# A graph layer's source terms: seven gathers per pair, the eighth tile by columns and rows, with a table made on chip

## What is computed

```python
msg_in = jnp.concatenate([x[src], x[dst], edge_attr_32], axis=-1)
messages = relu(msg_in @ mW1 + mb1) @ mW2 + mb2
aggregated = jax.ops.segment_sum(messages, dst, num_segments=12500)
upd_in = jnp.concatenate([x, aggregated], axis=-1)
y = x + relu(upd_in @ uW1 + ub1) @ uW2 + ub2
return layernorm(y)          # per node, no scale or shift, eps 1e-5
```

## Time and profile before

| | us |
|---|---|
| median of 3 runs (1914.49 to 1922.07) | 1921.44 |
| the profiled execution | 1922.22 |
| its span | 1920.4 |
| DVE busy | 1540.8 (80%) |
| POOL busy | 1431.4 (75%) |
| PE busy (matmuls) | 1429.3 (74%) |
| ACT busy | 1242.0 (65%) |
| DMA moved | 229.86 MB, 44% of the engines' time in the middle |

### The profile page before, as it was taken

One profiled execution on the slowest core, in us unless ns is written; L12 is line 12 of the kernel. 1 busy time (PEld: TensorE's weight loads), 2 busy tenths in 40 slices (PEclk: granted clock), 3 DMA queues, 4 the chain that ended last, 5 costly groups with the idle time before them and its releaser, 6 DMA issues.

```text
span 1920.4 us, 56413 instructions
## 1 busy us (share of the span) xinstructions
PE 1429.3 (74%) x8716; PEld 1334.2 (69%) x8716; DVE 1540.8 (80%) x10793; ACT 1242.0 (65%) x10165; POOL 1431.4 (75%) x1527
## 2 busy tenths in 40 slices
PE   6776677777678777767768777776867878777877
PEld 6776566777667677666667667766767767766776
DVE  5568888888888888888888888888888888888883
ACT  3246766767766766766666666766666666766663
POOL 7777777777777777777777777777777777777773
PEclk8898888778877878788887887878788776877686
DMA  9664444444444444444444444444444444444441
GB/s 239 163 154 113 123 114 114 123 115 114 123 113 114 124 115 112 120 118 113 115 123 113 112 122 117 114 119 120 112 115 123 113 114 122 115 114 119 118 109 35
DMA packets 169379, 229.86 MB, mean 120 GB/s; under 512 B 98508, under 2 KB 117687, under 8 KB 168701
## 3 DMA queue, kind: packets, MB, share of 16 engines
q1 hardware_dynamic: 112484, 124.14, 23.4%
q0 software_dynamic: 48416, 97.68, 20.6%
q10 hardware_dynamic: 8254, 5.59, 1.2%
HBM read 217.59 MB, written 9.60 MB: 118 GB/s over the span
## 4 chain that ended last, share of the span: by engine, by line
POOL 63%; issue 23%; PE 4%; DVE 3%; DMA 3%; DVEq 1%; ACT 1%; POOLq 1%; SPq 1%; ACTq 0%
POOL gath L717 63%; DVE col_x L469 2%; DMA gath<-table_src,idx 1%; PE ps_sum L856 1%; DVEq L460 1%; DMA table_src<-gath 1%; PE ps_pre L824 1%; PE ps_pre L825 1%; DVE hid L1180 1%; PE ps_pre L790 0%; PE ps_pre L832 0%; POOLq L302 0%; DMA xwin<-in_xT_dram 0%; ACT hid L1000 0%; DMA col_src<-in_srcT_dram 0%
## 5 line engine op out<-in xcount | busy, mean ns | idle before, releaser
L717 POOL DMA_INDIRECT gath<-table_src,idx x1388 | 1309.6, 944 | 423.0 <-issue 420.6
L469 ACT COPY col_x<-xdeg 64x1 f32 x9428 | 912.4, 187 | 237.6 <-issue 219.6
L832 PE MATMUL ps_pre<-rhs,lhs 128*128 128x128 f32 x3226 | 603.0, 363 | 448.3 <-DVE lhs L1158 445.6
L469 DVE COPY col_x<-xdeg 64x1 f32 x9408 | 718.2, 138 | 216.0 <-issue 215.5
L832 PEld LDWEIGHTS ps_pre<-rhs,lhs 128*128 128x128 f32 x3226 | 558.8, 269 | 477.1 <-DVE lhs L1158 473.9
L856 PE MATMUL ps_sum<-onehot,hid 128*128 128x96 f32 x3322 | 473.2, 304 | 13.0 <-ACT rhs L976 11.9
L856 PEld LDWEIGHTS ps_sum<-onehot,hid 128*128 128x128 f32 x3322 | 463.3, 221 | 23.5 <-issue 15.2
L1007 ACT ACTIVATE hid<-hid 128x1024 f32<-128x1024 f32 x202 | 212.5, 1052 | 180.4 <-DVE hid L1180 177.0
L1180 DVE TENSOR_TENSOR hid<-ps_pre,gath 128x1024 f32<-128x1024 f32 x202 | 246.4, 1220 | 87.2 <-DMA gath<-table_src,idx 75.4
L1158 DVE TENSOR_SCALAR_CACHE_REDUCE lhs<-lhs,place 96x1024 f32<-96x1024 int32 x208 | 264.6, 1272 | 32.7 <-PE ps_sum L765 19.8
L1150 DVE TENSOR_TENSOR onehot<-ps_iota,dst_rel 128x768 f32<-128x768 f32 (+1 forms) x209 | 196.9, 943 | 0.1
(11 more groups left out here) (109 smaller groups left out, 639.1 us busy)
## 6 DMA issues: line engine op xcount, KB each, us to landing
lhs<-in_dst_dram SPq DMA_DIRECT2D x207, 384.0 KB
lhs<-in_edgeT_dram SPq DMA_DIRECT2D x207, 128.0 KB
gath<-table_src,idx POOLq DMA_INDIRECT x1388
table_src<-gath SPq DMA_DIRECT2D x12, 512.0 KB, 7.0
xwin<-in_xT_dram SPq DMA_DIRECT2D x208, 24.0 KB
idx<-in_srcT_dram SPq DMA_DIRECT2D x192, 4.0 KB
out_dram<-yout ACTq DMA_DIRECT2D x48, 64.0 KB, 1.6
col_src<-in_srcT_dram SPq DMA_DIRECT2D x148, 0.5 KB
```

The lines of the kernel that those rows point to most:

```text
L469: ins = copy(col_x[:, i, start + n + j:start + n + j + 1], col)
L717: pool.indirect_dma_start(gath[0:m, k, j * H:(j + 1) * H], None, table_src, src_by_tile(p, k, j, m)).then_inc(gathered[k], 16)
L832: mm = nc.tensor.matmul(to[0:m, j * H:(j + 1) * H], lhs[:, k, j * P:j * P + m], rhs[:, k, :], start=True, stop=not by_cols)
```

## The change

- **Programs.** `pairs` writes all iterations out for all engines; no loop is left.
- **Gathers.** All source numbers are loaded once into `idx_all` (pairs 0 to 15 early as before, the rest by one DMA); `idx` and its loads at each step go. From pair 13 to 206 every pair has seven gathers, slot 0 too. The last pair keeps three.
- **Eighth tile.** Its 128 edges are split: 8 by rows, 64 columns by ACT, 56 by DVE (24 and 32). For the rows SP issues eight DMAs per pair, each one row of `table_src` (512 B) into one partition of `gath`'s eighth tile, whose other partitions are set to zero once per slot; the first 8 columns of `col_x` are zero. `add_gathered` waits for the rows and adds eight tiles, as before.
- **Numbers.** `col_src` and its DMAs go. At steps 6 to 8 DVE copies the eighth tiles' numbers out of `idx_all`, PE turns them by two transposes, and DVE writes them as integers to `col_tab`, columns 8 to 127 multiplied by 4, so that they are byte offsets into `xdeg`. `column` uses them without a multiplication. `COL_GROUP` is 6.
- **Register loads.** ACT loads 16 at a time, the first 16 of a pair a step ahead; DVE 24 and 32; SP 8. The window's starts are loaded four at a time by DVE (`load_starts`) and SP.
- **Order.** At step p ACT copies all 64 columns of pair p + 2, after relu. DVE copies 32 of pair p + 1 between onehot and the compare, and 24 of pair p + 2 at the end; the addresses for the sums are resolved (`place_sums`) ahead of the first batch. SP issues the rows of p + 3 last, behind a wait for `hsum_made` of p - 1.

The diff, cut to its core:

```diff
-PEELED = 4
-COL_K = (1, 2, 3)
-COL_FIRST = 3
+EARLY = 16
+COL_FROM = 13
 COL_TILE = PT - 1
-COL_HALF = P // 2
-COL_GROUP = 3
-COL_PLAN = (((2, 0, 32), (1, 48, 16)), ((2, 32, 32), (0, 0, 16)), ((0, 16, 32), (0, 48, 16)), ((1, 0, 32), (1, 32, 16)))
-COL_BATCHES = (3, 3, 2)
+COL_ROWS = 8
+COL_ACT = 64
+COL_LOAD = 16
+COL_DVE = 24
+COL_GROUP = 6
+DVE_FROM = COL_ROWS + COL_ACT
+WORD = 4
+COL_MADE = 6
+TAB = (PAIRS + 2) // 2
 LAST_ROWS = TILES - 1
-LAST_COLS = ((2, LAST_ROWS, P), (0, TILES, TAIL))
...
-        def pairs(eng, step, node, tail, peeled=PEELED, looped=True):
-
-
-            for it in range(peeled if looped else LAG):
+        def pairs(eng, step, node, tail):
+            for it in range(ITERS - 1):
...
+        def gathers_of(p):
+            return rows_of(p) if is_last(p) else PT - has_cols(p)
...
+        def load_regs(eng, p, start, count):
+            row, half = p % TAB, p // TAB
             regs = [eng.alloc_register(f"col{next(col_regs)}") for n in range(count)]
+            for n in range(0, count, 32):
+                eng.load(regs[n:n + 32], col_tab[row:row + 1, half, start + n:start + min(n + 32, count)])
+            return regs
+        def column(eng, reg, scaled):
+            if not scaled:
+                return xdeg[0:D, bass.ds(eng.snap(reg, donate=True, min_val=0, max_val=N - 1), 1)]
+            at = eng.snap(reg, donate=True, min_val=0, max_val=(N - 1) * WORD, out_of_modulus=WORD)
+            return xdeg[0:D, :].bitcast(U8)[:, bass.ds(at, WORD)].bitcast(F32)
+        def copy_batch(eng, copy, k, start, regs):
+            for n in range(0, len(regs), COL_GROUP):
+                of = [column(eng, reg, start + n + j >= COL_ROWS) for j, reg in enumerate(regs[n:n + COL_GROUP])]
                 for col in of:
                     eng.lower_ap(col)
                 for j, col in enumerate(of):
+                    ins = copy(col_x[:, k, start + n + j:start + n + j + 1], col)
+            return ins
+        def wait_cols(eng, p):
+            if p == COL_FROM:
+                eng.wait_ge(cols_tabled, 4)
+            if col_before(p) is not None:
+                eng.wait_ge(pe_steps, steps_for_pre(col_before(p)))
+            let(eng)
+        def src_by_tile(p, j, m):
...
+                if (it, k) == (0, 2):
+                    sp.dma_start(idx_all[:, EARLY * PT:], srcT[:, EARLY * PT:PAIRS * PT]).then_inc(idx_last_in, 16)
                 if pair(it, k, -SLOTS):
                     load_window(*pair(it, k, -SLOTS))
                 if pair(it, k, -PREP):
                     load_pair(*pair(it, k, -PREP))
+                p = it * SLOTS + k
+                if has_rows(p + PREP):
+                    load_rows(p + PREP, (k + PREP) % SLOTS)
+            def load_rows(p, k):
+                if p == COL_FROM:
+                    sp.wait_ge(cols_tabled, 4)
+                sp.wait_ge(hsum_made, p - SLOTS + 1)
+                if not has_rows(p - SLOTS):
+                    sp.wait_ge(gath_zero, p - COL_FROM + 1)
+                let(sp)
+                for n, reg in enumerate(load_regs(sp, p, 0, COL_ROWS)):
+                    src = sp.snap(reg, donate=True, min_val=0, max_val=N - 1)
+                    sp.dma_start(gath[n:n + 1, k, COL_TILE * H:PW], table_src[bass.ds(src, 1), :]).then_inc(rows_in[k], 16)
...
-                if not (isinstance(p, int) and p < RAW + SLOTS):
+                if p >= RAW + SLOTS:
                     pool.wait_ge(hsum_made, p - SLOTS + 1)
-                if not p_early(p):
-                    pool.wait_ge(idx_in[k], (it - PEELED + 1) * 16)
+                if p == EARLY:
+                    pool.wait_ge(idx_last_in, 16)
                 let(pool)
-                for j, m in tiles_of(p):
-                    if j == rows_of(p) or j == COL_TILE and has_cols(it, k):
-                        break
-                    pool.indirect_dma_start(gath[0:m, k, j * H:(j + 1) * H], None, table_src, src_by_tile(p, k, j, m)).then_inc(gathered[k], 16)
+                for j, m in tiles_of(p)[0:gathers_of(p)]:
+                    pool.indirect_dma_start(gath[0:m, k, j * H:(j + 1) * H], None, table_src, src_by_tile(p, j, m)).then_inc(gathered[k], 16)
...
+                        if p == COL_FROM:
+                            pe.wait_ge(col_zero, 1)
+                        if j == col_tile(p):
+                            pe.wait_ge(cols_act, col_batches(p) + is_last(p))
+                            pe.wait_ge(cols_dve, 2 * col_batches(p))
+                        of = col_x[:, k if j == col_tile(p) else PAIRS % SLOTS, 0:m]
...
+                p = it * SLOTS + k
+                to = (k + 2) % SLOTS
+                if has_cols(p + 2):
+                    if p + 2 == COL_FROM:
+                        first_regs(p + 2)
+                    held = act_regs.pop() + load_regs(act, p + 2, COL_ROWS + COL_LOAD, COL_LOAD)
+                    copy_batch(act, nc.scalar.copy, to, COL_ROWS, held)
+                    for start in range(COL_ROWS + 2 * COL_LOAD, DVE_FROM, COL_LOAD):
+                        done = copy_batch(act, nc.scalar.copy, to, start, load_regs(act, p + 2, start, COL_LOAD))
+                    done.then_inc(cols_act, 1)
+                if p + 2 >= COL_FROM and has_cols(p + 3):
+                    first_regs(p + 3)
...
+                dve.wait_ge(gathered[k], got(p))
+                if has_rows(p):
+                    dve.wait_ge(rows_in[k], rows_got(p))
...
+            def load_starts(p):
+                regs = [dve.alloc_register(f"start{p + i}") for i in range(SLOTS)]
+                dve.load(regs, start_i[0:1, p:p + SLOTS])
+                starts.update((p + i, reg) for i, reg in enumerate(regs))
+            def place_sums(p):
+                at = bass.ds(dve.snap(starts.pop(p), donate=True, min_val=0, max_val=WMAX), WIN)
+                dve.lower_ap(agg[:, at])
+                dve.lower_ap(xdeg[D:D + 1, at])
+                return at
...
-                copy_cols(dve, nc.vector.tensor_copy, it, k, 0, COL_HALF, cols_dve)
+                p = it * SLOTS + k
+                if p % SLOTS == SLOTS - 1:
+                    load_starts(p - SLOTS + 1)
+                at = place_sums(p - 3) if p >= 3 else None
+                if p == COL_MADE:
+                    dve.wait_ge(idx_last_in, 16)
+                    for at_f, at_i in ((slice(0, LAST_PAIR), slice(COL_TILE, LAST_PAIR * PT, PT)),
+                                       (slice(LAST_PAIR, 2 * TAB), slice(LAST_PAIR * PT + LAST_ROWS, LAST_PAIR * PT + LAST_ROWS + 2 * TAB - LAST_PAIR))):
+                        nc.vector.tensor_copy(col_f[:, at_f], idx_all[:, at_i]).then_inc(cols_listed, 1)
+                if p == COL_MADE + 2:
+                    dve.wait_ge(cols_turned, 1)
+                    for half in range(2):
+                        for at_c, scale in ((slice(0, COL_ROWS), 1.0), (slice(COL_ROWS, P), float(WORD))):
+                            nc.vector.tensor_scalar(col_tab[0:TAB, half, at_c], ps_node[0:TAB, half * P + at_c.start:half * P + at_c.stop],
+                                                    scale, None, ALU.mult).then_inc(cols_tabled, 1)
+                if has_cols(p + 1):
+                    to, start = (k + 1) % SLOTS, DVE_FROM + COL_DVE
+                    done = copy_batch(dve, nc.vector.tensor_copy, to, start, load_regs(dve, p + 1, start, P - start))
+                    if is_last(p + 1):
+                        done = copy_batch(dve, nc.vector.tensor_copy, to, 0, load_regs(dve, p + 1, 0, COL_ROWS))
+                    done.then_inc(cols_dve, 1)
+                if has_cols(p + 2):
+                    wait_cols(dve, p + 2)
                 after_this = pair(it, k, -1)
-                if after_this and not (isinstance(it, int) and after_this[0] < 2):
+                if after_this and after_this[0] >= 2:
                     turned(*after_this)
                 if pair(it, k, 3):
-                    add_sums(*pair(it, k, 3))
-                if isinstance(it, int) and (it, k) == (COL_FIRST, 0):
-                    dve.wait_ge(hsum_made, COL_FIRST * SLOTS)
-                    for i in COL_K:
-                        nc.vector.memset(gath[:, i, COL_TILE * H:PW], 0.0).then_inc(col_zero, 1)
-                copy_cols(dve, nc.vector.tensor_copy, it, k, 1, COL_HALF, cols_dve)
-                if isinstance(it, int) and (it, k) == (ITERS - 1, 1):
-                    copy_last(dve, nc.vector.tensor_copy, 2, COL_HALF, COL_HALF // 2, cols_dve)
-                    copy_batch(dve, nc.vector.tensor_copy, 2, COL_HALF + COL_HALF // 2, COL_HALF // 2, cols_dve)
+                    add_sums(*pair(it, k, 3), at)
+                if has_cols(p + 2):
+                    to = (k + 2) % SLOTS
+                    held = load_regs(dve, p + 2, DVE_FROM, COL_DVE)
+                    copy_batch(dve, nc.vector.tensor_copy, to, DVE_FROM, held).then_inc(cols_dve, 1)
```

More of the change, by code:

```diff
@@ L25 @@
 I32 = mybir.dt.int32
+U8 = mybir.dt.uint8
 ALU = mybir.AluOpType
@@ L200, in gnn_kernel @@
```

(55 more changed lines are left out.)

162 lines of the change are left out of this document (52 added, 110 removed).

## The result

| | before | after |
|---|---|---|
| median of four runs each, side by side (us) | 1919.29 | **1860.05** (1857.16 to 1869.49) |
| ratio to before, with its 95% interval | | **0.9702** [0.9661, 0.9744] |
| profiled execution: time, span (us) | 1922.2, 1920.4 | 1858.6, 1856.8 |
| gathers in all, 0.944 us each in the middle | 1465 (1388 of them in the earlier trace rows) | 1417 |
| last gather ends, and what follows it (us) | 1896.27, 24.1 | 1838.16, 18.6 |

59 us faster, where 24 were forecast. It is the time of the rival "POOL stays the bound", 1862. First the page of the changed kernel: the chain that ended last, its costliest groups, and a DMA issue group.

What follows compares the result with a forecast made beforehand. POOL bounds the kernel before; the bound passes to DVE, whose terms take 8.60 to 8.93 us a pair against POOL's 8.74. Over 193 steps that saves 24.4 us from 1922.2: 1898 us, range 1860 to 1942.

Steps and rivals of the forecast that it cites:

- POOL stays the bound: Rival: DVE needs under 8.74 us a pair, so POOL's gathers still set the pace; 1862 us, chance 0.24.
- What bounds, and what a gather costs: POOL bounds the kernel before; one gather costs 1.248 us with issue, so 48 fewer save at most 59.9 us.
- DVE's columns: DVE copies 56 columns a pair instead of 48, at 69 ns each instead of 73.4: +0.34 us a pair.
- The start's loads: DVE's window start loaded by fours: -0.53 load, -0.18 check and resolving, +0.17 new load, +0.07 resolving, us a pair.
- the load of 24: DVE's second batch loads 24 registers instead of 16: +0.42 us a pair.
- the waits that go: DVE's three waits ahead of a first batch, in three steps of four, disappear: 0.11 us a pair saved.
- The two waits ahead of the compare: Two added DVE sequencer instructions for the column buffer; with one for the rows, 0.15 us a pair.
- The register loads: On DVE, 0.48 us a load plus 0.052 us a register, split from two sequencer stretches.
- 8.6 to 9.0: ACT's need in us a pair with 64 columns, before any breaks within batches.
- the breaks that the rival needed for its 9.2: Written-out ACT gets DVE's mid-batch breaks, needs up to 9.2 us a pair: 1950 us; chance 0.18 with DVE over 9.11.
- SP late: Rival: SP's eight row copies at 0.76 us each make 9.55 us a pair, 2017 us; decides from 0.70; chance 0.04.
- No change: Rival: DVE's single start load is cheap (-0.2 for -0.53), 9.0 to 9.1 us a pair, 1910 to 1930 us; chance 0.14.

## Why the prediction was wrong

**What bounds, and what a gather costs: right.** The last gather ended 58.1 us earlier (1896.27 to 1838.16), forecast 48 x 1.248 = 59.9 as the most there is. The other part of the 63.6 us between the spans is the end, 24.1 to 18.6 us, which I had as unchanged. DVE has 0.57 us a pair of slack where it had 0.38, so it may stand nearer to POOL when that stops; this is argued, not shown.

**DVE's columns: the step that failed.** "I take 69, nearest to the rows' own sum", and "70 ns, or 66 if the resolving hides altogether". Measured: 61. I had split the 73.4 ns into 66 of copy and 7 of resolving, from three copies in 0.27 us, and took off only what the larger group saves. The multiplication, which the change names in its own table, I gave nothing. But the 73.4 was the sequencer's pace, 74 ns a column, above an engine that needs 60.4. Without the multiplication the sequencer needs 62 in groups of three and 52 in groups of six, so it keeps up, and the batch has the engine's pace; with it, groups of six would have left 73. The 4 ns for the grouping were wrong as well: with the multiplication in place the sequencer gains 1 by it, and without it the columns gain 1.4 (62.4 to 61), since there the engine is the floor. 56 x (69 - 61) = 0.45 us a pair of the 0.76 between 8.93 and 8.17. This term alone brings 8.93 to 8.48, under POOL's 8.74, and so turns the bound round.

**The other 0.3** can be laid out with the help of the version with the start loaded at every step (one profiled execution, means over all pairs). The start's loads brought 0.08 more than forecast, the load of 24 cost 0.05 more. The stretch from hid to the first column grew by 0.14, forecast 0.13; but its two parts were +0.38 for +0.24 and a remainder of -0.24 where I had the waits that go at -0.11, so that agreement is luck, and the waits, if the remainder is theirs, brought 0.13 more. The two waits ahead of the compare (0.10) and the one for the rows (0.05) show as nothing, and the breaks within batches fell by 0.07. Some 0.04 go the other way, as the need before was 8.64 and not 8.60. These parts without the columns' price would alone have brought DVE to about 8.62, under 8.74 too. So the column term is the largest, but either half was enough.

**The register loads.** The price of 0.48 us a load and 0.052 a register was a split of two stretches, and the kernel before's own trace has the loads by themselves: 0.31 us for one register, where the split gives 0.53; 1.10 for 16, where it gives 1.31; 2.10 for 32, close to its 2.15. In the sum the errors cancel in large part: the single start load came out near (0.55 for 0.47), with the check and the resolving dearer than I had them and the load cheaper.

**ACT:** "8.6 to 9.0", measured 8.44 to 8.47. A column costs (4.73 - 0.187)/47 = 97 ns where I had 93; the second and third load show 0.15 and 0.21, not 0.26 and more, and the breaks that the rival needed for its 9.2 didn't come. It is the nearest behind POOL, and the rival's mechanism is the next bound, 0.3 us further down than its price. **SP late:** 0.40 a row, its threshold was 0.70.

**No change** asked for a cheap start load (9.26) less luck: that part turned out dear (0.92 with its check), and the columns cheap. That the rival "POOL stays the bound" needed "every one of DVE's terms" to "fall well" was wrong too: one that was misread sufficed. The range's lower end was that rival's floor, and the median, 1860.05, lies on it. With 2% between two engines' sums, and one term of 56 copies that came out 8 ns off (0.45 us, 5% of the period), the two cases should have stood about even.

## What to carry to other kernels

A stream of small instructions with addresses from registers has two paces, the engine's and its sequencer's. Look in the trace for a batch that starts with the sequencer ahead (after the engine was held up): if its copies lie closer than usual, the engine isn't what they cost, and arithmetic on addresses (a multiplication by the element size) is worth a table of ready numbers. The sequencer's register loads and register arithmetic stand in the trace with their times, under the line that makes them: read them there before splitting a stretch by hand.

Where two engines' needs are within a few per cent, a change that gives one of them work costs nothing as long as its need stays under the other's; here a need that comes near showed first in what follows the last work of the bound engine, not in the period (18.6 us in the change and 19.6 with columns from pair 11, DVE's need at 8.2 in both; 26.3 with DVE at 8.72; 29.1 with groups of three; one profiled execution each).

## What the runs showed of the hardware

- The kernel before took 1920 us on two of the chips given to the experiments and 3020 to 3070 on three others, each steady to about 1.5%. There, copies come singly after idle times of 0.56 or 1.2 us, with issue alone before them. The change brought 3% on the first kind; with groups of three, 2% on the second; and the version with columns in three slots of four brought 7% there. It has the fewest instructions of those run (50,936 by its page, against 56,413 before and 59,577 after), but the kernel before with seven gathers has 56,365 and gains 2%, and the groups of three and the unscaled version have 63,478 each, of which the first gains 2% and the second nothing. The count alone doesn't order them, and the cause stays open.
- Eight row DMAs of 0.5 KB, each with an address from a register, were issued in 3.16 us, 0.40 each, less than the 0.46 between plain neighbouring issues in the earlier trace rows.
- A register load from SBUF took DVE's sequencer 0.31 us for one register (in the changed kernel with the start loaded at every step, 73 of 180 took 0.53), 0.35 or 0.57 for four, 0.61 for eight, 1.10 for 16, 1.64 for 24 and 2.10 to 2.16 for 32 (medians): from eight registers on some 63 ns each, with little fixed beside it.
